# Convolution taps read from SBUF instead of PSUM, and an x-projection accumulated block by block, in a Mamba block between two feed-forward blocks

## The reference

```python
proj = jnp.einsum('blh,oh->bol', x, W_in)
h, gate = jnp.split(proj, 2, axis=1)          # 1024 channels each
conv = lax.conv_general_dilated(h, conv_w[:, None, :], window_strides=(1,), padding=[(K - 1, 0)],
                                feature_group_count=I, ...)   # K = 4 taps, causal, per channel
h = jax.nn.silu(conv + conv_b[None, :, None])
ssm_p = jnp.einsum('bil,oi->blo', h, Wx)      # the x-projection: 128 + 16 + 16 columns
ts, Bm, Cm = jnp.split(ssm_p, [R, R + N], axis=-1)
```

## Time and profile before

| | |
|---|---|
| time, median of 3 runs | 3078.54 us (3074.34 to 3086.39) |
| profiled execution, its own time | 3078.0 us |
| its span, first to last instruction | 3076.2 us |
| granted TensorE clock, mean | 0.893 |
| busy VectorE / TensorE / GpSimd / ScalarE | 85% / 80% / 68% / 54% |
| HBM traffic over the span | 197 GB/s |

### The profile page before, as it was taken

How to read it: one execution, slowest core, us unless ns; L and a number is a source line. 1 busy time by engine, 2 the same in 40 slices (tenths; PEclk the granted TensorE clock), 3 DMA queues, 4 the chain that set the end, 5 groups by cost and what they waited for, 6 DMA issues and landing times. The chain is left out here.

```text
span 3076.2 us, 37111 instructions
## 1 busy us (share of the span) xinstructions
PE 2449.2 (80%) x12266; PEld 1987.2 (65%) x12266; DVE 2604.1 (85%) x3289; ACT 1675.2 (54%) x2789; POOL 2100.1 (68%) x1240
## 2 busy tenths in 40 slices
PE   7577666967877789779986799879987797788768
PEld 5466555746666678667765677658766575676546
DVE  5529898989999888799988898899997888899962
ACT  5446446565745655656645556656654556645422
POOL 2226747776975678768875688768885579877722
PEclk9769897978889999899988899889998898898878
DMA  7634552664487456956586366865577365665524
GB/s 270 237 112 138 180 200 67 198 238 161 129 287 253 138 190 214 325 182 205 179 292 230 106 198 210 285 246 162 189 246 271 103 226 198 221 231 196 191 76 134
DMA packets 294951, 608.68 MB, mean 198 GB/s; under 512 B 23008, under 2 KB 23776, under 8 KB 294752
## 3 DMA queue, kind: packets, MB, share of 16 engines
q1 hardware_dynamic: 294752, 606.23, 58.3%
HBM read 453.57 MB, written 152.57 MB: 197 GB/s over the span
## 5 line engine op out<-in xcount | busy, mean ns | idle before, releaser
L1002 POOL TENSOR_TENSOR sbuf<-dus,bring 128x1024 f32<-128x1024 f32 x512 | 1216.8, 2394 | 393.5 <-PE pt L1042 248.2
L502 PE MATMUL pm<-xT,wring 128*128 128x512 f32 x4352 | 1142.8, 413 | 152.5 <-DVE hd L706 68.0
L502 PEld LDWEIGHTS pm<-xT,wring 128*128 128x128 f32 x4352 | 835.7, 198 | 335.6 <-issue 146.4
L1016 ACT ACTIVATE pa<-dls,cst 128x512 f32<-128x512 f32 x1024 | 692.7, 687 | 582.1 <-DVE sbuf L1025 544.8
L1042 PE MATMUL pt<-ident,sbuf 128*128 128x128 f32 x4096 | 675.4, 306 | 299.1 <-DVE sbuf L1025 230.0
L1042 PEld LDWEIGHTS pt<-ident,sbuf 128*128 128x128 f32 x4096 | 528.4, 157 | 455.4 <-DVE sbuf L1025 286.2
L1053 DVE SCALAR_TENSOR_TENSOR acc<-pt,cT,acc 128x512 f32<-128x512 f32 x896 | 638.2, 741 | 101.3 <-PE pt L1042 95.8
L1025 DVE TENSOR_TENSOR_SCAN sbuf<-pa,sbuf 128x512 f32<-128x512 f32 x512 | 607.4, 1210 | 79.2 <-ACT pa L1016 51.4
L1025 DVE TENSOR_TENSOR_SCAN sbuf<-pa,carry,sbuf 128x512 f32<-128x512 f32 x512 | 635.4, 1270 | 13.7 <-ACT pa L1016 13.2
L574 PE MATMUL pm<-wring,act 128*128 128x512 f32 x2176 | 587.6, 413 | 36.5 <-DVE hd L939 16.9
L574 PEld LDWEIGHTS pm<-wring,act 128*128 128x128 f32 x2176 | 407.4, 195 | 129.9 <-DVE hd L939 19.8
(11 more groups left out here) (123 smaller groups left out, 2022.5 us busy)
## 6 DMA issues: line engine op xcount, KB each, us to landing
wring<-wsp SPq DMA_DIRECT2D x408, 512.0 KB, 4.3
bring<-b_d SPq DMA_DIRECT2D x256, 256.0 KB, 3.8
xn_d<-tb SPq DMA_DIRECT2D x24, 1024.0 KB, 9.3
xnb<-xn_d SPq DMA_DIRECT2D x21, 1024.0 KB, 7.2
x_d<-tb SPq DMA_DIRECT2D x16, 1024.0 KB, 5.9
u_d<-hd SPq DMA_DIRECT2D x64, 256.0 KB, 2.9
sg_d<-hd SPq DMA_DIRECT2D x64, 256.0 KB, 2.8
tb<-x_d SPq DMA_DIRECT2D x16, 1024.0 KB, 7.1
```

The lines of the kernel that those rows point to most:

```text
L502: f = lambda e, pw=pw, px=px, k=k, first=(i == 1), end=(i == total): e.matmul(pm[b][:, 0:n], lhs(pw, k), rhs(px, k), start=first, stop=end)
L1002: t_p = S.op("pool", lambda e, s2=s2, s3=s3, h=h: e.tensor_tensor(sbuf[:, s3, h * m:(h + 1) * m, :], dus[:, h * m:(h + 1) * m, :], bring[: ...
L1016: t_e = S.op("act", lambda e, k=k, i=i, pb=pb, n=n: e.activation(pa[pb][:, :], dls[:, k, :], ACT.Exp, scale=col(C_A + i * N + n)), dl_tok[ ...
```

## The change

1. In the convolution ScalarE copies the projected row from its PSUM bank into an SBUF row `xb` with three columns in front for the halo. Three such rows lie in the tile `xnb`, used in turn. In odd chunks the three halo columns come from `hsave` by a small ScalarE copy; in even chunks the taps leave the first columns out as before. `hfix` and its GpSimd operations go, and so does the VectorE correction; `hsave` is now written by ScalarE.
2. The taps read `xb` and `a`, both in SBUF. The tanh is written into `xb` and the product with it reads `xb` and `a`. The PSUM bank is free after ScalarE's reads of it.
3. The x-projection is accumulated block by block: two of the four `pm` banks are held during the convolution, each for two groups of 128 tokens (160 columns each), and for each block, two blocks behind (`XLAG`), 12 matmuls of 160 columns are issued. Two blocks' share remains after the convolution. The ScalarE copy behind it handles two groups at once.
4. `prefetch` is called after the convolution, and the last gate product stands before the rest of the x-projection.

The diff, cut to its core:

```diff
--- before.py
+++ after.py
@@ -13,6 +13,7 @@
 N = 16
 J = 11
 R = 128
+XW = R + 2 * N
 HALO = 3
 SLOTS = 3
 DWELL = 12.0
@@ -25,15 +26,14 @@
 PEF = 1.12
 
 LAG = 3
+XLAG = 2
 
 CUT = 2
 NT = 2
 
...
 
 GU, DN, WIN, WO = 0, 2 * J, 3 * J, 3 * J + 16
 NPIECE = 3 * J + 16 + 8
@@ -238,7 +238,6 @@
         mhalf = sb("mhalf", [P, 12])
         mone = sb("mone", [P, 1])
         hsave = sb("hsave", [P, NI, 4])
-        hfix = sb("hfix", [P, NI, 8])
         cst = sb("cst", [P, NCONST])
         csh = sb("csh", [P, 11 + 11 + 4 + 40])
         lnw = sb("lnw", [P, 2 * N])
@@ -484,7 +483,11 @@
             bank_n = [begun.get("bank_n", 0)]
             bank_free = list(begun.get("bank_free", [()] * (6 - NT)))
 
+            held = set()
+
             def bank():
+                while bank_n[0] % (6 - NT) in held:
+                    bank_n[0] += 1
                 b = bank_n[0] % (6 - NT)
                 bank_n[0] += 1
                 return b, bank_free[b]
@@ -679,34 +682,25 @@
                 t_xT = make_xT(t_in, src)
                 if c + 1 < NCH:
                     pre_norm(free, ln_out, c + 1)
-                prefetch(0 if c == 0 else 1)
                 u_tok, g_tok = [], []
-                if not even:
-                    cw4 = csh[:, H_CW:H_CW + 4 * NI].rearrange("p (i k) -> p i k", k=4)
-                    at = {3: 0, 2: 4, 1: 6}
-                    for k in (3, 2, 1):
-                        t_fix = C.op("pool", lambda e, k=k: e.tensor_tensor(
-                            hfix[:, :, at[k]:at[k] + k], hsave[:, :, HALO - k:HALO],
-                            cw4[:, :, 3 - k:4 - k].broadcast_to([P, NI, k]), ALU.mult),
-                            *(hs_tok if k == 3 else ()), *freed("hfix"), n=8)
-                    for k in (2, 1):
-                        t_fix = C.op("pool", lambda e, k=k: e.tensor_tensor(
-                            hfix[:, :, 0:k], hfix[:, :, 0:k], hfix[:, :, at[k]:at[k] + k], ALU.add), t_fix, n=8)
-                    free["hsave"] = (t_fix,)
-                opened = []
+                opened, x_ready_of = [], {}
+                xbanks = [bank() for h in range(2)]
+                held.update(b for b, w in xbanks)
 
                 a_buf = aa[:, 0, :], aa[:, 1, :], th[:, 0, :]
                 a_key = ("aa", 0), ("aa", 1), ("th", 0)
+                xrow = xnb[:, :, :].rearrange("p a n -> p (a n)")
+                x_buf = [xrow[:, 520 * s:520 * s + HALO + TC] for s in range(3)]
+                x_free = [freed("xnb")] * 3
 
                 def finish():
 
-                    i, r, b, t_c = opened.pop()
-                    a = a_buf[i % 3]
-                    t_th = C.op("act", lambda e: e.activation(pm[b][:, :], a, ACT.Tanh), t_c, table="tanh")
+                    i, r, t_c = opened.pop()
+                    a, xb = a_buf[i % 3], x_buf[i % 3]
+                    t_th = C.op("act", lambda e: e.activation(xb[:, HALO:HALO + TC], a, ACT.Tanh), t_c, table="tanh")
                     t_u = C.op("dve", lambda e: e.scalar_tensor_tensor(
-                        hd[:, r, :], pm[b][:, :], 1.0, a, ALU.add, ALU.mult), t_th, *freed(("hd", r)))
-                    free[a_key[i % 3]] = (t_u,)
-                    bank_free[b] = (t_u,)
+                        hd[:, r, :], xb[:, HALO:HALO + TC], 1.0, a, ALU.add, ALU.mult), t_th, *freed(("hd", r)))
+                    free[a_key[i % 3]] = x_free[i % 3] = (t_u,)
                     t_hi = C.op("act", lambda e: e.activation(act[:, 0, i, :], hd[:, r, :], ACT.Copy),
                                 t_u, *freed("act"))
                     t_lo = C.op("pool", lambda e: e.tensor_tensor(
@@ -714,40 +708,67 @@
                     t_st = C.dma(st_u[r], u_d[c, i], hd[:, r, :], t_u)
                     u_tok.append(t_st)
                     free["hd", r] = (t_hi, t_lo, t_st)
-                    return t_hi, t_lo
-
+                    x_ready_of[i] = t_hi, t_lo
+
+                def x_step(k):
+
+                    for tt in range(4):
+                        b, w = xbanks[tt // 2]
+                        for pw, px in PARTS:
+                            i, end = (pw, px) == PARTS[0], (pw, px) == PARTS[-1]
+                            first_here = i and k == 0 and tt % 2 == 0
+                            f = lambda e, b=b, tt=tt, pw=pw, px=px, start=first_here, stop=(end and k == NI - 1): e.matmul(
+                                pm[b][:, (tt % 2) * XW:(tt % 2 + 1) * XW], act[:, pw, k, tt * P:(tt + 1) * P],
+                                wxs[:, px, k, :], start=start, stop=stop, skip_group_check=True)
+                            ws = (*x_ready_of[k], t_small[0]) if i and tt == 0 else ()
+                            t = M.matmul(f, *ws, *(w if first_here else ()), n=XW, last=end and (tt % 2 == 1))
+                            if end and k == NI - 1 and tt % 2 == 1:
+                                x_done.append((b, t))
+
+                x_done = []
                 for i in range(NI):
-                    r, a = i % 2, a_buf[i % 3]
+                    r, a, xb = i % 2, a_buf[i % 3], x_buf[i % 3]
                     slot, t_w = piece(WIN + i)
                     b, w = bank()
                     t = gemm(b, slot, t_w, w, t_xT)
                     cw = lambda k, i=i: hc(H_CW + 4 * i + k)
+                    if not even:
+                        C.op("act", lambda e, xb=xb, i=i: e.activation(xb[:, 0:HALO], hsave[:, i, 0:HALO], ACT.Copy),
+                             hs_tok[i], *x_free[i % 3], n=3)
+                    C.op("act", lambda e, b=b, xb=xb: e.activation(xb[:, HALO:HALO + TC], pm[b][:, :], ACT.Copy),
+                         t, *x_free[i % 3])
                     t_c = C.op("act", lambda e, b=b, a=a, i=i, cw=cw: e.activation(
                         a, pm[b][:, :], ACT.Identity, bias=hc(H_CB + i), scale=cw(3)),
                         t, *freed(a_key[i % 3]), more=0.1)
+                    bank_free[b] = (t_c,)
                     if even:
-                        hs_tok[i] = C.op("dve", lambda e, b=b, i=i: e.tensor_copy(
-                            hsave[:, i, 0:HALO], pm[b][:, TC - HALO:TC]), t_c, *freed("hsave"), n=1)
-                    else:
-                        t_c = C.op("dve", lambda e, i=i, a=a: e.tensor_tensor(
-                            a[:, 0:HALO], a[:, 0:HALO], hfix[:, i, 0:HALO], ALU.add), t_c, t_fix, n=1)
-                        free["hfix"] = (t_c,)
+                        hs_tok[i] = C.op("act", lambda e, b=b, i=i: e.activation(
+                            hsave[:, i, 0:HALO], pm[b][:, TC - HALO:TC], ACT.Copy), t, n=3)
+                        bank_free[b] = (hs_tok[i],)
                     for k in range(1, 4):
-                        t_c = C.op("dve", lambda e, b=b, a=a, k=k, cw=cw: e.scalar_tensor_tensor(
-                            a[:, k:TC], pm[b][:, 0:TC - k], cw(3 - k), a[:, k:TC], ALU.mult, ALU.add),
+                        lo = k if even else 0
+                        t_c = C.op("dve", lambda e, xb=xb, a=a, k=k, lo=lo, cw=cw: e.scalar_tensor_tensor(
+                            a[:, lo:TC], xb[:, HALO - k + lo:HALO - k + TC], cw(3 - k), a[:, lo:TC], ALU.mult, ALU.add),
                             t_c, more=0.06)
                     if opened:
                         finish()
-                    opened.append((i, r, b, t_c))
+                    opened.append((i, r, t_c))
                     if c and i < NI - 2:
                         g_tok.append(gate(c, i, t_xT))
-                t_hi, t_lo = finish()
+                    if i >= XLAG:
+                        x_step(i - XLAG)
+                finish()
+                free["xnb"] = tuple(t for f in x_free for t in f)
+                prefetch(0 if c == 0 else 1)
                 if c:
                     g_tok.append(gate(c, NI - 2, t_xT))
+                    g_tok.append(gate(c, NI - 1, t_xT))
                 post_ready[c] = (u_tok, g_tok)
                 xT_tok[c] = t_xT
-                late = [lambda: g_tok.append(gate(c, NI - 1, t_xT))] if c else []
-                x_proj(c, t_hi, t_lo, late)
+                for k in range(NI - XLAG, NI):
+                    x_step(k)
+                free["act"] = (x_done[-1][1],)
+                x_proj(c, x_done)
 
             def gates(c):
 
@@ -772,23 +793,20 @@
                 free["xT"] = (t,)
                 return t_st
 
-            def x_proj(c, t_hi, t_lo, late):
-
-                for tt in range(4):
-                    b, w = bank()
-                    t = mm(b, lambda p, k, tt=tt: act[:, p, k, tt * P:(tt + 1) * P],
-                           lambda p, k: wxs[:, p, k, :], NI, R + 2 * N, (*w, t_hi, t_lo, t_small[0]))
-                    t_s = M.op("act", lambda e, b=b, tt=tt: e.activation(
-                        ssb[:, tt, :], pm[b][:, 0:R + 2 * N], ACT.Copy), t, *freed("ssb"), n=160)
-                    t_q = None
-                    for a, (lo, hi_) in enumerate(((0, R), (R, R + N), (R + N, R + 2 * N))):
```

(23 more changed lines are left out.)

## The result

The changed kernel takes 3097.97 us (median of 4 runs, 3095.67 to 3102.63) against 3076.44 us before, measured beside it: a ratio of 1.0061, 95% interval 1.0037 to 1.0085. It is slower by 0.6%, some 19 us by the ratio, where the prediction said 61 us. The size was wrong.

The account below looks back on a forecast made before the run. VectorE, 90% busy in the convolution windows after the first, was taken to set the pace. Waits and removed work +86, projection -15, banks -10 made +61 us on 3078.0, about 3140 us, range 3045 to 3265.

Parts of the forecast that it names:

- (b): Convolution, chunks 1 to 7: 224 taps and products wait for GpSimd 0.69 us each, 155 us; bounds 67 and 284.
- (c): VectorE loses lines 732 and 729, 50 us; nine tenths of its net +95 us reach the end, +86 us.
- (g): Convolution banks: two held for projection, others freed after ScalarE's reads; -10 us, between 0 and -30.
- (a): Taps and gate product read SBUF: undisturbed tap falls from 742 to about 688 ns, 10 us gained; product stays.
- (d): GpSimd held back up to 0.69 us at each of 224 operations, up to 155 us, nothing at first given its idle time.
- (e): ScalarE gains 64 PSUM copies and 64 small ones, 51 us, covered by idle time; 5 us in the opening without cover.
- (f): Projection accumulated block by block: three quarters of the first chunk's 20.7 us leave the path, -15 us; other chunks nothing.
- (h): Load of the next normalised rows moves behind the convolution: costs nothing, or 49 us if its cover were gone.
- The first rival: Nearly every exposed tap and product waits for GpSimd like line 732: +224 us less 25, 3277 us; chance 22%.
- half-rate arithmetic: Taps and products with two fp32 SBUF inputs run at half rate: 138 us on top, some 3265 us; chance 3%.
- my forecast's condition: Waits of taps and products for GpSimd of 0.45 to 1 us, giving 3090 to 3200 us; chance 48%.
- the two cancel: Waits of taps and products near 0.4 us balance the gains: 3065 to 3090 us; chance 11%.

Follow-up runs that it names:

- acc_psum: sbuf_only with the sum `a` in the PSUM bank, held until the product, so each tap reads one SBUF and one PSUM tensor; 3078.55 us, ratio 0.9996.
- sbuf_held: sbuf_only with the PSUM bank held until the product instead of freed after ScalarE's reads; 3168.94 us, ratio 1.0289.
- sbuf_only: Kernel before with only the SBUF rows for taps, tanh and product, bank freed after ScalarE's reads, old projection, four banks; 3104.81 us, ratio 1.0077.
- xlag8: Changed kernel with its whole projection in one piece behind the convolution, still in two held banks; 3091.44 us, ratio 1.0033.
- halo_act: Kernel before without line 732, its three halo columns corrected by one-column ScalarE operations; 3069.65 us, ratio 0.9958.
- tanh_sbuf: halo_kmajor with the tanh written to an SBUF row and the bank released after the third tap; 3009.91 us, ratio 0.9787.
- halo_kmajor: halo_act with the projection summed block by block in two banks, wholly behind the convolution; 3061.03 us, ratio 0.9937.
- before_chain: Kernel before with four VectorE statistics operations behind each tap-chain block's taps in chunks 1 to 7, unknown to the planner; 3286.93 us, ratio 1.0666.
- dummy_planned: Kernel before with 224 added VectorE operations in the chain of taps, without waits for GpSimd, their length told to the planner; 3299.99 us, ratio 1.0712.
- after_told: Changed kernel with the planner told that each tap and product takes 0.47 us longer in chunks 1 to 7; 3157.36 us, ratio 1.0257.

## Why the prediction was wrong

The way from one kernel to the other, from the ratios: the rows in SBUF with the sum in PSUM, which takes line 732 away and adds ScalarE's copies, 0 (acc_psum); the waits for GpSimd in a held chain, +90 (sbuf_held); the early release, -65 (sbuf_only); the projection in block order behind the convolution, in two banks, and the moved gate, -14 (xlag8); its accumulation within the convolution, +9. Sum +20, measured +19. The steps' prices hang on the order in which they are taken, and each carries its own planned order.

Beside the prediction's terms, each with its nine tenths, this gives: the wait 90 us and not 140; no tap gain, which was to give 9; nothing for lines 732 and 729, which were to give 45; 5 us for the projection and not 15; 65 us for the banks and not 10. The errors are -50, +9, +45, +10 and -55, in sum the 41 us by which the forecast of +61 was too high. Three steps failed: the size of the wait (b), the rate of exchange (c) and the size of the banks' gain (g).

- **(a) tap gain of 10 us: none.** The undisturbed tap stays at 0.74 us (median 745 ns). Line 385's 688 ns were the wrong row: it has no weight read from memory, as the taps have. In the earlier trace rows lines 736 and 706, both reading PSUM, already differ by 64 ns in that way.
- **(b) the wait: right in kind, mis-sized by 58 us.** It is there, it alternates as told, but at 0.43 us and not 0.69: 97 us, not 155. A wait that happens has the forecast length (97 us over 80 operations, 1.2 us each) and GpSimd is busy 56% of the changed kernel's convolution windows, as the forecast's 58% had it. What was wrong is how often an operation meets it: 79 of 224 or 35%, not 58%. Why is not shown (perhaps GpSimd runs where VectorE is busy with the scan). The bound from today's places (0.30) was the nearer row.
- **(c) "I let nine tenths reach the end": failed as a rule.** Taking 41 us away from VectorE gave 13 us (halo_act) or nothing (acc_psum), where nine tenths would be 37. Waits of 89 us cost 90 (sbuf_held), and 89 us of added operations cost 0.5, 1.1 or 2.3 times their length, new orders included. I read 90% busy as a rate of exchange, and no one rate fits these.
- **(d), (e): right.** GpSimd's busy time rises by 18 us and its product averages 2420 ns, not 2394. ScalarE has 30 us more to do (51 forecast); acc_psum carries all its copies and costs nothing in sum.
- **(f) -15 us: the opening gained 7**, and for another reason, block order. The stretch from the last tap of the first chunk to the first scan shrank by 17 us, from 61.7 to 44.9, but it is as short in xlag8 (45.0), and with the matmuls within the convolution that last tap starts at 160.5 us and not at 150.4 (154.7 in xlag8). So the placement within the convolution, which the sum rested on, gives nothing.
- **(g) banks at -10, bounded by -30: mis-sized by 55 us.** The release is worth 65 us with waiting taps, and tanh_sbuf shows 46 us with taps that don't wait, each with its new order. I took the 68.0 us of the earlier trace rows for idle time of an engine that isn't the bound. But in TensorE's fixed order the matmul that waits for the bank has others behind it, the scan's transposes among them, which VectorE and GpSimd need. That this is the path of the gain is argued and not shown: GpSimd waits longer for the transposes in both kernels with the early release (315.3 us in sbuf_only, 281.2 in sbuf_held; 286.7 in tanh_sbuf, 264.1 in halo_kmajor), and these are the faster ones.
- **(h): right.** TensorE waits 7.6 us for `xnb`. The DMA queue's waits on the product have grown from 87.7 to 160.3 us without TensorE or the scans showing it.

With the measured wait and no tap gain, my own sum (97 - 50 us by 0.9, less 25) gives +17, about what was measured. So the wait's size alone makes the number wrong. That the rest comes out is luck: the errors in (c) and (g) cancel. The first rival (all wait like line 732) and half-rate arithmetic didn't happen. The wait of 0.43 us falls just under my forecast's condition (0.45 to 1 us), beside that of "the two cancel" (near 0.4), whose times, 3065 to 3090 us, are passed by 8 us.

What remains open is why a microsecond of waiting costs 1.0 in sbuf_held but one of work 2.3 in before_chain. One difference is on record: in before_chain the planner sees the added operations as links and puts 96 more scans between the taps, while the waits of sbuf_held are in no plan (162 scans, 175 in acc_psum). A run of the added operations in the old order would test it.

## What to carry to other kernels

A VectorE operation with two SBUF inputs pays for GpSimd's long ones, which shows as a mean far above the median (1.13 against 0.75 us over all taps here). Price such a wait by how often it is met and not only by how long it lasts. Before pricing time on a busy engine, ask what its end releases: the same four operations per block cost 205 us in the chain that holds a PSUM bank, 94 where the bank was free already and 43 behind the chain. Where a planner orders the kernel, compare the orders too before such a price is believed. Here the good part of the change (giving the bank back early) can be had with one operation in four waiting for GpSimd; with the halo correction on ScalarE and the projection in block order, which bring about 20 of its 66 us, that beats both kernels.

## What the runs showed that was not expected

In every one of the 15 kernels the profiled execution ends 118 to 121 us after its last scan begins, so a change counts by what it does to the scans. The changed kernel starts its last tap at 2344 us, 76 us before the kernel before does, and is slower all the same: its scans lag behind, those of chunk 4 begin at 1667 us and not at 1597.

The copies of the rows by ScalarE, all else that acc_psum changes included, cost some 12 us, by which halo_act, without line 732 and without the copies, is faster than it. TensorE's wait for the bank does not measure the loss: it grows by 96 us in dummy_planned beside 219 us, and by 51 in before_chain (119.0 us) beside 205. And correct costs given to the planner made the order worse by 60 us (after_told), so a plan that models more is not therefore a better one.
